# One attention exponential of 2048 columns or two of 1024, with the score banks used in halves

## The reference, cut to what matters

```python
x = x + 0.5 * ffn(layernorm(x), w_gate, w_up, w_down)
q, k, v = (xn @ Wq + bq), (xn @ Wk + bk), (xn @ Wv + bv)    # xn = layernorm(x) * g + b
attn = einsum('bnhd,bmhd->bnmh', q, k) / sqrt(64)
y = einsum('bnmh,bmhd->bnhd', softmax(attn, axis=2), v)
x = x + y
x = x + 0.5 * ffn(layernorm(x), w_gate, w_up, w_down)
```

## Time and profile before

| | us |
|---|---|
| median of 3 runs | 5026.3 |
| lowest and highest | 5019.46, 5246.73 |
| the profiled execution | 5018.85 |
| span of its slowest core (core 5) | 5017.3 |
| spans of all cores | 4996.4 to 5017.3 |
| busy: TensorE matmul | 3719.8 (74%) |
| busy: ScalarE | 1398.1 (28%) |
| busy: VectorE | 1046.6 (21%) |

### The profile page before, as it was taken

How to read it: one execution, slowest core, us unless ns; L and a number is a source line. 1 busy time by engine, 2 the same in 40 slices (tenths; PEclk the granted TensorE clock), 3 DMA queues, 4 the chain that set the end, 5 groups by cost and what they waited for, 6 DMA issues and landing times. The chain is left out here.

```text
span 5017.3 us, 55981 instructions; the slowest of 8 cores (4996.4 to 5017.3 us)
## 1 busy us (share of the span) xinstructions
PE 3719.8 (74%) x22790; PEld 1757.3 (35%) x22790; DVE 1046.6 (21%) x1686; ACT 1398.1 (28%) x1192; POOL 143.7 (3%) x267
## 2 busy tenths in 40 slices
PE   3399795875666666697988979687666666659799
PEld 2244342332333333343434434233233333334344
DVE  3421312332000000312212121233200000022211
ACT  0011111003666666211111111000366666621110
POOL 3200001000000000000000000100000000000000
PEclk9699897986555555798999989788755555569899
DMA  8823214000000000332222322410000000023221
GB/s 248 255 68 118 76 55 113 17 9 17 1 34 9 26 34 1 95 115 85 76 73 70 118 76 56 104 34 9 17 1 34 1 34 34 1 84 118 84 76 42
DMA packets 264651, 316.12 MB, mean 63 GB/s; under 512 B 8904, under 2 KB 205512, under 8 KB 263376
## 3 DMA queue, kind: packets, MB, share of 16 engines
q1 hardware_dynamic: 238160, 230.74, 15.9%
q0 software_dynamic: 26240, 81.80, 5.3%
HBM read 255.89 MB, written 69.21 MB: 65 GB/s over the span
## 5 line engine op out<-in xcount | busy, mean ns | idle before, releaser
L904 ACT ACTIVATE att_eS<-PS,cb 128x2048 bf16<-128x2048 f32 x512 | 1007.1, 1967 | 654.9 <-PE PS L890 654.9
L890 PE MATMUL PS<-Q,K 64*128 64x512 bf16 x2048 | 531.3, 612 | 640.7 <-ACT att_eS L904 639.9
L819 PEld LDWEIGHTS PS<-V,att_eS 128*128 128x128 bf16 x8192 | 457.4, 130 | 420.5 <-issue 420.5
L819 PE MATMUL PS<-V,att_eS 128*128 128x65 bf16 x8192 | 538.4, 243 | 5.2 <-DVE att_x2b L851 5.2
L438 PE MATMUL PS<-a1s_xnfm,a1s_wslg 128*128 128x512 bf16 x1536 | 368.9, 384 | 0.0
L438 PE MATMUL PS<-cs_xnfm,cs_wslg 128*128 128x512 bf16 x1536 | 368.3, 383 | 0.0
L444 PE MATMUL PS<-a1s_xnfm,a1s_wslu 128*128 128x512 bf16 x1536 | 363.7, 380 | 0.0
L444 PE MATMUL PS<-cs_xnfm,cs_wslu 128*128 128x512 bf16 x1536 | 363.6, 380 | 0.0
L482 PE MATMUL PS<-a1s_wdsb,a1s_hsb 128*128 128x512 bf16 x1536 | 332.2, 379 | 7.5 <-DVE a1s_hsb L461 7.5
L482 PE MATMUL PS<-cs_wdsb,cs_hsb 128*128 128x512 bf16 x1536 | 332.2, 379 | 7.5 <-DVE cs_hsb L461 7.5
L890 PEld LDWEIGHTS PS<-Q,K 64*128 64x128 bf16 x2048 | 82.1, 104 | 722.0 <-issue 722.0
(11 more groups left out here) (109 smaller groups left out, 2112.2 us busy)
## 6 DMA issues: line engine op xcount, KB each, us to landing
a1s_wslg<-wgT SPq DMA_DIRECT2D x48, 512.0 KB, 4.1
a1s_wslu<-wuT SPq DMA_DIRECT2D x48, 512.0 KB, 5.4
cs_wslg<-wgT SPq DMA_DIRECT2D x48, 512.0 KB, 4.2
cs_wslu<-wuT SPq DMA_DIRECT2D x48, 512.0 KB, 5.5
a1s_xst<-L_attn_x SPq DMA_DIRECT2D x32, 512.0 KB, 6.3
x1s<-a1s_xo POOLq DMA_DIRECT2D x32, 512.0 KB, 5.1
a2s_xst<-x1s SPq DMA_DIRECT2D x32, 512.0 KB, 3.3
att_x1q<-x1s SPq DMA_DIRECT2D x8, 2048.0 KB
```

The costliest lines, as they stand in the source:

```text
L819: inst = e.matmul(PS1[:, (par * 2 + q2) * 512: (par * 2 + q2) * 512 + 65], expS[:, buf + kt * 1024 + par * 512 + qt * 128: buf + kt * 1024 ...
L890: inst = e.matmul(PS0[:, pp + par * 512: pp + (par + 1) * 512], K_sb[64 * par:64 * par + 64, hp * 2048 + r * 128: hp * 2048 + (r + 1) * 12 ...
L904: "scalar", lambda e, hp=hp, rr=rr, buf=buf: e.activation(expS[:, buf + rr * 2048: buf + (rr + 1) * 2048], PS0[:, 0:2048], AF.Exp, bias=cb ...
```

## The change

The round of two blocks is given up: the loop runs over the 16 blocks `r`. Each block's two score matmuls write two banks of `PS0` (banks 0 and 1 for even r, 2 and 3 for odd), and a ScalarE exponential of 1024 columns reads those two banks. A block's matmuls wait for the exponential two blocks back, `exp_last[r % 2]`. The V chunk is emitted after each odd block, as before once in two blocks. The dependency of a V chunk on the last exponential of its pair is renamed from index 7 to index 15. Beside this, the copy of the four sums becomes a maximum with 1e-30.

```diff
-                deps = [t_exp[(qg, hp, 7)]]
+                deps = [t_exp[(qg, hp, 15)]]
...
-                    t_l = ph.op("vector", lambda e, qtp=qtp: e.tensor_copy(
-                        lbuf[:, qtp * 4: qtp * 4 + 4][:, :, None],
-                        PS1[:, :].rearrange("p (a t) -> p a t", a=4)[:, :, 64:65]),
+                    t_l = ph.op("vector", lambda e, qtp=qtp: e.tensor_scalar(
+                        out=lbuf[:, qtp * 4: qtp * 4 + 4][:, :, None],
+                        in0=PS1[:, :].rearrange("p (a t) -> p a t", a=4)[:, :, 64:65],
+                        scalar1=1e-30, scalar2=None, op0=ALU.max),
...
-                    for rr in range(8):
-                        for kk in range(2):
-                            r = rr * 2 + kk
-                            pp = (r % 2) * 1024
+                    for r in range(16):
+                        pp = (r % 2) * 1024
...
-                            t_mm = ph.op("tensor", st_fn,
-                                         deps=[exp_last[0]], inc="mm")
-                        t_exp[(qg, hp, rr)] = ph.op(
-                            "scalar", lambda e, hp=hp, rr=rr, buf=buf: e.activation(
-                                expS[:, buf + rr * 2048: buf + (rr + 1) * 2048],
-                                PS0[:, 0:2048], AF.Exp,
+                        t_mm = ph.op("tensor", st_fn, deps=[exp_last[r % 2]],
+                                     inc="mm")
+                        t_exp[(qg, hp, r)] = ph.op(
+                            "scalar", lambda e, hp=hp, r=r, buf=buf, pp=pp: e.activation(
+                                expS[:, buf + r * 1024: buf + (r + 1) * 1024],
+                                PS0[:, pp:pp + 1024], AF.Exp,
                                 bias=cb8[:, hp:hp + 1], scale=0.125),
                             deps=[t_mm, pv_war[hp % 2], t_cb], inc="sc")
-                        exp_last[0] = t_exp[(qg, hp, rr)]
-                        if pend[0] is not None:
-                            emit_pv_chunk(pend[0][0], pend[0][1], rr)
+                        exp_last[r % 2] = t_exp[(qg, hp, r)]
+                        if pend[0] is not None and r % 2 == 1:
+                            emit_pv_chunk(pend[0][0], pend[0][1], r // 2)
```

More of the change, by code:

```diff
@@ new lines, in attn_phase, with st_fn @@
+                    for r in range(16):
+                        pp = (r % 2) * 1024
+                        def st_fn(e, hp=hp, r=r, qg=qg, pp=pp):
+                            for par in range(2):
+                                inst = e.matmul(
+                                    PS0[:, pp + par * 512: pp + (par + 1) * 512],
+                                    K_sb[64 * par:64 * par + 64,
+                                         hp * 2048 + r * 128:
+                                         hp * 2048 + (r + 1) * 128],
+                                    Q_sb[64 * par:64 * par + 64,
+                                         hp * 2048 + qg * 512:
+                                         hp * 2048 + (qg + 1) * 512],
+                                    start=True, stop=True)
+                            return inst
+                        t_mm = ph.op("tensor", st_fn, deps=[exp_last[r % 2]],
[4 more added lines that the diff above has]
+                                PS0[:, pp:pp + 1024], AF.Exp,
```

## The result

The changed kernel takes 4403.6 us (median of 10 runs) where the kernel before takes 5026.1 (median of 10). The ratio is 0.878, with a 95% interval of 0.875 to 0.881, so it is 12% faster. The profiled execution took 4399.9 us, and the spans of its cores are 4380.5 to 4398.3.

A forecast was written before the change was run, and what follows sets the result against it. ScalarE's exponentials and TensorE's score matmuls wait for each other, 3.25 us a round. Falling to 2.12 gains 1.13 x 512 = 579 us, less 7 lost: 4447 from 5018.9, forecast median 4445, range 4390 to 4520.

The forecast's parts named there:

- my own case: Attention loop: TensorE's clock at both levels in turn, mean round 2.12 us, kernel 4415 to 4480 us; chance 0.45.
- rival 2: Attention loop: TensorE stays at 2.4 GHz and ScalarE alone decides, round 2.04 us, kernel 4404 us; chance 0.20.
- The round of 3.25 us, nothing overlapping: Old attention loop: exponential 1.97, gap 0.14, score matmuls 1.04, gap 0.10 us, one after the other.
- ScalarE's term: Attention exponentials of 1024 columns: 1.115 us each, 0.095 overlap, spacing 1.02, so 2.04 us for a round (1.97 to 2.42).
- a sign of being wrong: Attention exponentials: a mean duration over 1.2 us was to show the prediction wrong; near 1.115 was to show it right.
- rival 3: Attention exponentials stand 0.10 us apart instead of overlapping by 0.095: round 2.42 us, kernel 4594 us; chance 0.07.
- The chain at 1.2 GHz: Attention: odd exponential, scores, V chunk, even scores, next odd exponential sum to 4.395 us over two rounds, 2.20 for one.
- The clock: TensorE in attention: a rise to 2.4 GHz likely, then a fall likely again; mean round 2.12 us, between 2.04 and 2.20.
- The sum's last step: Whole kernel: from 4447 us for the profiled execution to a median of 4445, expected the same within a few us.
- VectorE's handing over: After V chunks 3 and 7: takes 1.33 us, costed at nothing; without cover 0.19 x 128 = 24 us.
- The adds: After each query group: adds and stores make chunk 3's copy about 1.3 us late, three times a phase, 7 us lost.
- The maximum and the renamed dependency: VectorE's maximum for the sums' copy: at most 3 us if on the path; dependency 7 to 15: nothing.

The follow-up runs named there:

- V chunks in pairs: The changed kernel with the V chunks emitted two at a time, after every fourth block: 4624 and 4627 us, ratio 0.917 to the kernel before.
- V pieces: The changed kernel with each V chunk cut into two pieces of 8 matmuls, one behind each block's scores: 4430 and 4435 us.
- cut exponential: The changed kernel with each exponential on 512 of its 1024 columns, all matmuls kept: 4161 to 4171 us.
- six-bank version: The changed kernel with V results packed and 1536-column exponentials from two three-bank buffers: 4402 to 4412 us; with V matmuls starting one unit later, 4342 to 4345 us.
- serial kernel: The changed kernel with every block's score matmuls waiting for the exponential just before them, not two back: 5377 to 5389 us.
- three-buffer kernel: The changed kernel with packed V banks and three two-bank score buffers in place of two, exponentials still 1024 columns: 4382 and 4386 us.

## Why the prediction was right, and where it was off

The direction, the mechanism and the range (4390 to 4520) hold. 4445 is 41 us above the 4404 measured, outside the 4415 to 4480 of my own case. That case, both levels in turn, is what the traces show, but its time is that of rival 2, the upper level throughout, to which I gave 0.20. That rival's 4404 to the microsecond is luck: its round of 2.04 was ScalarE's 2.04 without a pause, and the measured 2.04 is 2.01 with pauses.

- *The round of 3.25 us, nothing overlapping.* Right. Halves without overlap cost 1.97 each, where the sum with the same terms says 1.965.
- *ScalarE's term.* The duration of 1.115 from two other rows was right within a nanosecond for an exponential that stands alone. In the changed kernel the mean is 1.198, just under the 1.2 that I had called a sign of being wrong; the spacing of the starts shows that this was a poor sign. The spacing was 1.005 in place of 1.02, since the overlap is 0.11 and not 0.095: 0.03 for a round, 15 us of the 41. The upper bound with a gap (rival 3) is out: no gap shows in 847 instructions. The Trainium skill, ScalarE: Activation LUTs, "What ACT_TABLE_LOAD costs", gives 1.133 less 0.093, a spacing of 1.04; the trace has 1.005.
- *The chain at 1.2 GHz.* Right in kind, as the kernel with V chunks in pairs shows. It is 2.26 and not 2.20: from a V chunk to the scores behind it takes 1201.03 - 1200.03 = 1.00 where I took 0.87 between bounds of 0.82 and 1.06. With 1.00 the sum is 4.395 + 0.13 = 4.525, over two 2.26.
- *The clock.* This is the term that was off. I said that it would rise, which it did, 12 us after the first V chunks, and that it would fall again for so much of the time that the mean round is 2.12, the middle of 2.04 and 2.20, for which I had no working. The mean round is 523.35 / 256 = 2.04. The clock does fall, but for a round or two, and then the round costs 2.26 instead of 2.01, so that a fall shows as a pause of 0.2 to 0.4. I had argued the fall from the norms' matmuls, which are denser than the loop, and yet the loop kept 1.00 for 29 us (19.59 busy in 29.00 against 4.79 in 6.30); no row of before told where between the two levels it would sit. A mean clock of 0.92 puts 16% of the phase at the lower level, where my middle had half. By my own 2.04 and 2.20 that is a round of 2.07, 0.05 less than 2.12, or about 26 us; the spacing's 15 are the other part of the 41.
- *The sum's last step.* The working ends at 4447 for the profiled execution, which took 4399.9. The 47 between them are these 41 and the adds' 7, which the measured 2.04 already holds. The step from 4447 to 4445 had no reason: the median before lies 7 us above its profiled execution, and not below it.
- *The Trainium skill's rule,* TensorE: Matmul & The Clock Gate, "Why this matters for your kernels", that only long gaps bring the clock down, was nearer to the outcome (0.92) than my case. It is still not borne out: with pauses of only 0.61 the changed kernel falls to 0.50 now and then. My own argument against it, that the old loop never rose, was no evidence, since the rule speaks of when the clock falls.
- *VectorE's handing over.* Right as costed, at nothing: TensorE's wait for it is 8.0 us in all, in the group of L819, and 5.1 of them are the four waits of 1.27 behind the phases' last rounds, which the kernel before had too (5.2). The V pieces and the cut exponential show what it costs without cover.
- *The adds.* Three late places in each phase, as said. Chunk 4 of the first waited 0.79 us for L852, and ScalarE then 0.39; I had 1.2 for each. 7 us was too much, since a buffer of scores lay between:

```profile
1338.63 0.65 PE L819 MATMUL PS<-V,att_eS 128*128 128x65 bf16 x16 [0.79 <-DVE att_x2b L852]
...
1339.70 6.14 ACT L903 ACTIVATE att_eS<-PS,cb 128x1024 bf16<-128x1024 f32 x6 [0.39 <-PE PS L889]
```

- *The maximum and the renamed dependency.* The maximum costs nothing, as said and measured. The renamed dependency names the same data and has no run of its own.

## What to carry to other kernels

Where two engines hand one buffer back and forth, halve it and let each wait for the step two back; then count one more instruction's fixed part as the price (here 0.15 to 0.18 us on a round that fell from 3.25 to 2.01 at the upper clock). Look next at what stands in the producer's order between the two halves: here the chain of exponential, scores, V chunk and next scores decides when the producer is slow, and a third buffer takes it out. Once one engine has no pause left, only fewer and wider instructions on it help, and they pay only if the other engine keeps its slack, which the six-bank version shows by failing first and then giving 57 us.

## What the runs showed of the hardware that I had not expected

- Exponentials that follow each other are recorded with a mean of 1.198 us, those of the serial kernel with 1.115, and yet they start 1.005 apart. In the three-buffer kernel the mean is 1.412 at the same spacing. So a mean duration of queued ScalarE instructions is not their cost; the spacing of starts is.
- The clock of TensorE changed from 0.50 over two whole phases to 0.92 though TensorE had the same matmuls to do; they came in 534 us in place of 842. Which of the two came first can't be told from that alone. What the trace shows is that at the lower level TensorE was nearly without a pause before the rise (11.29 busy in 12.00), while the kernel before idled 1.21 in each round and never rose.
- A step that gained nothing in one order (six banks, 4402) gained 57 us in another that moved the V matmuls of each head pair behind one more unit of scores.
